# Causal attention on TensorE: the two heads of a pair in the two row halves of the array, and operand stacks loaded one stage earlier

## The chip, the cores and the metric

One Trainium2 (trn2) chip, one core. The metric is the device time of one execution in microseconds (us). The kernel before ran three times: 6051.51, 6053.97 and 6059.97 us, median 6053.97 us.

## The reference

A small recurrent network of two kinds of layers over 4 sequences of 1024 tokens with 128 channels. The first part is a tiled attention, then a causal attention with rotary positions behind a layer norm and a short convolution, then a mixture of four experts, then a second causal attention without rotation; after that come six layers of local attention with a gated network. The change touches only the two causal attentions. What each of them computes, cut down:

```python
# B = 4 sequences, T = 1024 tokens, 16 heads of D = 8 channels
q, k, v = split(h @ attn_w)                       # per head
scores = jnp.einsum('bqhd,bkhd->bhqk', q, k) / jnp.sqrt(D)
causal = jnp.tril(jnp.ones((T, T), dtype=bool))
p = jax.nn.softmax(jnp.where(causal, scores, -1e30), axis=-1)
y = jnp.einsum('bhqk,bkhd->bqhd', p, v).reshape(B, T, C)
return y @ proj_w
```

## The kernel before, in words

Every layer is a stage: the five engines run their own programs, joined by semaphores, and a barrier of all engines ends the stage. The two causal attentions are the stages named ca0 and ca1 (function `causal_attention`, tiles ending in `_of_ca`). Each follows a stage `causal_inputs` (ci0, ci1), which projects queries, keys and values in 8 chunks of 512 tokens and writes queries and keys, each cut into three bf16 parts, to memory (`q_parts`, `k_parts`, the two DMAs of a chunk at line 469). ci0 rotates the values and takes longer per chunk than ci1.

The work of an attention stage goes by 16 groups: 4 sequences times 4 groups of 4 heads. For a group SyncE (SP) loads a stack of queries and a stack of keys: six products of the three parts (`PRODUCTS`), 8 rows each, lie one above the other in 48 of the 128 partitions, so that one bf16 matmul gives a nearly exact fp32 score of a head. Two further rows, from `SHIFT_ROW` = 64, hold the negated maximum of each query against ones in the keys, so the maximum is subtracted inside the same matmul. The rest of the 128 rows is zero. There are three slots of stacks (`RING_CA`). They are cleared at the start of the attention stage, slot 0 by VectorE (lines 843 to 846), slots 1 and 2 by GpSimd (lines 594 to 596), and only then loaded (lines 556 and 558, 13 DMAs per group).

TensorE does two things for each group with these stacks:

- Maxima, one group ahead: `maximum` (line 624) computes scores with queries as rows. A task fills one of two double banks of PSUM (`PAIR_BANK`), and VectorE reduces it (line 783). There are 20 tasks per group, of 4 heads with 128 or 256 keys or of 2 heads with 384 or 512. Where the tile lies on the diagonal, a second matmul of 128 columns adds the mask (line 627).
- Scores and weighted values: the group is walked in 12 units (`UNITS`; query half 0 with 4 key tiles, query half 1 with 8). `score` (line 677) computes keys by queries, one head per bank in a ring of three banks (`SCORE_BANKS`), with a mask matmul on the diagonal (line 680); ScalarE takes the exponential out of the bank (line 759, semaphore `raised`); `weigh` (line 691) multiplies with the values of the four heads, in four strips of 32 columns of the array, one unit late.

The order on TensorE is written out: scores of heads 0 and 1, then the tasks of `between(G, i, 0)`, scores of heads 2 and 3, `between(G, i, 1)`, then `weigh` of the unit before. `BETWEEN` says how many maxima tasks stand in each of the two places. At unit 8 the eight matmuls of `turn_rows` (line 635) turn the maxima of the next group into the two rows that SP places in its stack (line 564). In some units of the first two groups of a sequence the steps of `FINISH` (totals, spread, mix) of the sequence before are added.

The two waits the change touches: a score matmul of one head waits until the exponential that used its bank before, three heads back, is done, and each head raises `scored` by itself.

```python
for h in heads:
    n = (G * NU + i) * HG + h
    if n >= SCORE_BANKS:
        pe.wait_ge(raised, n - SCORE_BANKS + 1)
    to = ps[:, n % SCORE_BANKS, j:]
    last = nc.tensor.matmul(to, keys[:, h, kt * P:(kt + 1) * P], ...)
    if diagonal:
        last = nc.tensor.matmul(to[:, 0:P], k["ident_b"][:, :], ...)
    last.then_inc(scored, 1)
```

Of the kernel before, what the change touches and what calls it, by code (L numbers as in the profile page):

```python
# [13 lines left out]
P = 128  # L14
# [18 lines left out]
SHIFT_ROW = 64  # L33
STACK_LOADS = 16 * (2 * len(PRODUCTS) + 1)
# [339 lines left out]
def causal_inputs(nc, name, ps, h, weights, tables, q_parts, k_parts, vtok):  # L374
# [4 lines left out]
    with Stage(nc, name) as st:  # L379
# [6 lines left out]
        stored, v_out, chain = [st.sem(f"stored{n}") for n in range(4)], st.sem("v_out"), st.sem("chain")  # L386
        with nc.Block() as block:
# [76 lines left out]
            def _(sp):  # L464
                for c in range(NCH):
                    for n, dram in enumerate((q_parts, k_parts)):
                        slot = c % 2 * 2 + n
                        sp.wait_ge(low, 2 * c + n + 1)
                        sp.dma_start(dram[:, :, chunk(c)].rearrange("s p t -> p s t"),
                                     parts[:, slot]).then_inc(stored[slot], 16)  # L470
                for slot in range(4):
                    sp.wait_ge(stored[slot], 16 * (NCH // 2))

# [4 lines left out]
RING_CA = 3  # L478
# [34 lines left out]
def causal_attention(nc, name, ps, k, q_parts, k_parts, vtok, proj, out, residual):  # L513
# [6 lines left out]
    with Stage(nc, name) as st:  # L520
        stacks = [(st.sb(f"queries{s}", [P, HG, L], BF16), st.sb(f"keys{s}", [P, HG, L], BF16)) for s in range(RING_CA)]
# [5 lines left out]
        zeros = st.sb("zeros", [2, L], BF16)  # L527
# [3 lines left out]
        cleared, first_cleared, copied = st.sem("cleared"), st.sem("first_cleared"), st.sem("copied")  # L531
# [6 lines left out]
        def in_pair(n, heads, width):  # L538

            first = PAIR_BANK + n % 2 * 2  # L540
            if heads == HG and width == P:
                return ps[:, first:first + 1, :].rearrange("p a (h n) -> p (a h) n", n=P)
            if heads == HG:
                return ps[:, first:first + 2, :].rearrange("p a (h n) -> p (a h) n", n=width)
            return ps[:, first:first + 2, 0:width]

        with nc.Block() as block:

            @block.sync
            def _(sp):  # L550
                def load(G):
                    slot, first = G % RING_CA, G % GROUPS * HG * HD
                    for to, dram, side in zip(stacks[slot], (q_parts, k_parts), range(2)):
                        for r, product in enumerate(PRODUCTS):
                            of = dram[product[side], first:first + HG * HD, G // GROUPS * L:(G // GROUPS + 1) * L]
                            sp.dma_start(to[r * HD:(r + 1) * HD, :, :], of.rearrange("(h d) t -> d h t", d=HD))\
                                .then_inc(loaded[slot], 16)
                    sp.dma_start(stacks[slot][0][SHIFT_ROW:SHIFT_ROW + 2, :, :],
                                 zeros[:, :].unsqueeze(1).to_broadcast([2, HG, L])).then_inc(loaded[slot], 16)

                def place(G):
                    sp.wait_ge(rows_out, G + 1)
                    for h in range(HG):
                        sp.dma_start(stacks[G % RING_CA][0][SHIFT_ROW:SHIFT_ROW + 2, h, :], rows[2 * h:2 * h + 2, :])\
                            .then_inc(placed[G % RING_CA], 16)

                sp.wait_ge(first_cleared, 8)
                load(0)
                for G in range(1, RING_CA):
                    sp.wait_ge(cleared, 7 * G)  # L570
                    load(G)
                place(0)
                for G in range(ALL - 1):
                    if G and G + 2 < ALL:
                        sp.wait_ge(scored, HG * NU * G)
                        load(G + 2)
# [5 lines left out]
            def _(pool):  # L582
# [9 lines left out]
                for queries, keys in stacks[1:]:  # L592
                    for low in (QUAD, SHIFT_ROW, SHIFT_ROW + QUAD):
                        link(nc.gpsimd.memset(queries[low:low + QUAD, :, :], 0.0))  # L594
# [1045 lines left out]
```

## Time and profile before

| what | value |
|---|---|
| median of 3 runs | 6053.97 us (6051.51 to 6059.97) |
| the profiled execution | 6055.52 us, its span 6053.7 us |
| TensorE matmul (PE) busy | 5119.5 us, 85% of the span |
| VectorE (DVE) busy | 4008.1 us, 66% |
| ScalarE (ACT) busy | 3245.7 us, 54% |
| GpSimd (POOL) busy | 1801.1 us, 30% |
| ca0 | from the clearing at 461.9 us to the last exponential at 1094.5 us |
| ca1 | from 1686.9 us to 2319.9 us |

PE is the row of matmuls, PEld that of weight loads. A matmul's duration holds its way through the array, so consecutive matmuls overlap in the records: what one costs in a row of many is the distance of their starts. "128\*128" behind an operation is the part of the array it uses, rows by columns. In the timeline a row with x8 stands for eight instructions in a row, and its time is from the start of the first to the end of the last; the bracket at the end is the idle time before it and what ended it.

### The profile page before, as it was taken

Reading aid. Unit: us, or ns where it says so; the run is one execution under the profiler, and the core shown is the slowest. Engines: PE = TensorE matmul, PEld = TensorE weight load, DVE = VectorE, ACT = ScalarE, POOL = GpSimd, SP = SyncE. Lnnn points to the kernel's source line nnn. Section 1 sums busy time; section 2 is a strip of 40 time slices with the busy share of each in tenths; the row PEclk is TensorE's granted clock in tenths of the full one; section 3 lists DMA queues with packets and bytes.
Section 4 is the critical chain, followed back from the end, with each engine's and each line's share of the span. In section 5 each row is a group of like instructions: output and inputs, shape, how many; then the busy total and the mean of one; then the engine's idle time right before and its main releaser. Section 6 shows DMA issues by size and latency. Waiting matters only on the chain. (4 is left out here: it accounts for less than half of the span.)

```text
span 6053.7 us, 164948 instructions
## 1 busy us (share of the span) xinstructions
PE 5119.5 (85%) x72264; PEld 2980.0 (49%) x72592; DVE 4008.1 (66%) x4630; ACT 3245.7 (54%) x4392; POOL 1801.1 (30%) x1232
## 2 busy tenths in 40 slices
PE   6756999788769996998799979997999799979997
PEld 3422333333323332666366636663666366636663
DVE  5756666233366664887488748884888488848884
ACT  2323555322235554776377637763777367736773
POOL 0003000000030001555155515551555055505550
PEclk9988999899889998999899989998999899989998
DMA  0011110000011111111111111110111011101111
GB/s 24 0 48 33 23 23 18 21 0 0 29 39 23 24 21 38 38 38 34 34 39 39 34 33 38 38 38 32 38 38 38 30 37 38 39 31 37 37 37 40
DMA packets 87157, 186.93 MB, mean 31 GB/s; under 512 B 23216, under 2 KB 39088, under 8 KB 84272
## 3 DMA queue, kind: packets, MB, share of 16 engines
q1 hardware_dynamic: 86448, 176.44, 12.1%
q8 instruction: 572, 9.37, 0.6%
q14 instruction: 137, 1.12, 0.1%
HBM read 59.97 MB, written 14.68 MB: 12 GB/s over the span
## 5 line engine op out<-in xcount | busy, mean ns | idle before, releaser
L1327 POOL TENSOR_TENSOR part_of_local<-part_of_local,sine_of_local 128x512 f32<-128x512 f32 x768 | 960.2, 1273 | 1061.3 <-DVE sine_of_local L1264 1061.3
L783 DVE TENSOR_REDUCE top_of_ca<-ps 128x2 f32<-128x1024 f32 (+3 forms) x640 | 695.1, 1115 | 298.6 <-PE ps L627 207.2
L759 ACT ACTIVATE prob_of_ca<-ps 128x512 f32<-128x512 f32 (+3 forms) x1536 | 654.5, 495 | 422.6 <-PE ps L680 311.0
L1334 POOL TENSOR_TENSOR part_of_local<-part_of_local,inverse_of_local 128x1024 f32<-128x1024 f32 x384 | 722.5, 1903 | 139.7 <-DVE inverse_of_local L1296 139.7
L624 PE MATMUL ps<-keys_of_ca,queries_of_ca 128*128 128x512 bf16 (+3 forms) x1474 | 386.4, 332 | 180.6 <-DMA queries_of_ca<-zeros_of_ca 86.4
L1301 DVE TENSOR_REDUCE total_of_local<-prob_of_local 128x16 f32<-128x1024 f32 x192 | 234.3, 1220 | 421.2 <-ACT prob_of_local L1240 421.2
L1261 DVE TENSOR_TENSOR part_of_local<-ps,rope 128x1024 f32<-128x1024 f32 x384 | 466.2, 1214 | 40.7 <-ACT square_of_local L1208 40.7
L1264 DVE TENSOR_TENSOR sine_of_local<-ps,rope 128x1024 f32<-128x1024 f32 x384 | 465.7, 1213 | 0.0
L1100 PE MATMUL ps<-qkv,shifted 128*128 128x512 f32 x768 | 392.4, 635 | 82.1 <-POOL values_of_local L1337 78.5
L1110 PE MATMUL ps<-qkv,shifted 128*128 128x512 f32 x768 | 381.6, 620 | 84.9 <-ACT heads_out_of_local L1236 71.8
L677 PE MATMUL ps<-queries_of_ca,keys_of_ca 128*128 128x512 bf16 (+2 forms) x1464 | 404.0, 331 | 24.3 <-issue 10.8
L1186 PEld LDWEIGHTS ps<-prob_t_of_local,mixed_of_local 64*64 64x64 f32 x12288 | 335.0, 135 | 166.2 <-issue 156.7
L1195 PE MATMUL ps<-heads_out_of_local,wo 128*128 128x128 f32 x3072 | 387.6, 281 | 14.1 <-ACT heads_out_of_local L1236 13.7
L1186 PE MATMUL ps<-prob_t_of_local,mixed_of_local 64*64 64x32 f32 x12288 | 383.8, 221 | 16.0 <-issue 9.1
L1186 PE MATMUL ps<-prob_t_of_local,values_of_local 64*64 64x32 f32 x12288 | 382.0, 219 | 4.7 <-issue 4.2
L1195 PEld LDWEIGHTS ps<-heads_out_of_local,wo 128*128 128x128 f32 x3072 | 368.8, 197 | 16.8 <-ACT heads_out_of_local L1236 16.7
L1167 PE MATMUL ps<-qkv,shifted 128*64 128x512 f32 x1536 | 376.9, 607 | 0.1
L594 POOL MEMSET queries_of_ca<- 32x4096 bf16 x12 | 42.1, 3505 | 1106.1 <-POOLq L63 1105.5
L1226 ACT ACTIVATE keys_of_local<-ps 128x1024 f32<-128x1024 f32 x192 | 196.8, 1025 | 323.2 <-PE ps L1129 323.2
L1247 ACT ACTIVATE values_of_local<-ps 128x1024 f32<-128x1024 f32 x192 | 196.6, 1024 | 306.2 <-PE ps L1167 306.2
L1186 PEld LDWEIGHTS ps<-prob_t_of_local,values_of_local 64*64 64x64 f32 x12288 | 338.0, 135 | 6.8 <-issue 5.9
L691 PE MATMUL ps<-prob_of_ca,values_of_ca 128*32 128x512 f32 (+3 forms) x3072 | 332.5, 505 | 0.0
(207 smaller groups left out, 9928.3 us busy)
## 6 DMA issues: line engine op xcount, KB each, us to landing
mixed_of_local<-values_of_local SPq DMA_DIRECT2D x636, 128.0 KB, 2.4
mixed_of_local<-values_of_local SPq DMA_DIRECT2D x264, 64.0 KB, 2.0
queries_of_ca<-q_parts SPq DMA_DIRECT2D x192, 64.0 KB
keys_of_ca<-k_parts SPq DMA_DIRECT2D x192, 64.0 KB
qkv<-in_qkv SPq DMA_DIRECT2D x7, 1536.0 KB, 6.5
rope<-in_rope SPq DMA_DIRECT2D x7, 1024.0 KB, 9.0
q_parts<-parts_of_ci SPq DMA_DIRECT2D x16, 384.0 KB, 2.5
k_parts<-parts_of_ci SPq DMA_DIRECT2D x16, 384.0 KB, 2.5
```

Source lines behind the costliest of these rows:

```text
L624: last = nc.tensor.matmul(to[:, h, :], queries[:, first + h, qt * P:(qt + 1) * P], keys[:, first + h, lo:lo + width], start=True, stop=not ...
L677: last = nc.tensor.matmul(to, keys[:, h, kt * P:(kt + 1) * P], queries[:, h, qc * CH + j:(qc + 1) * CH], start=True, stop=not diagonal)
L759: nc.scalar.activation(prob[:, i % 2, h, j:], ps[:, n % SCORE_BANKS, j:], ACT.Exp, scale=scale).then_inc(raised, 1)
L783: nc.vector.reduce_max(top[:, slot, first:first + heads], in_pair(n, heads, width), AX_X)\
L1100: last = nc.tensor.matmul(two_banks(SCORE_SLOT)[:, a, :], xs[:, tokens(t)], w["qkv"][:, 0, chunk(a)], start=True, stop=True)
L1110: last = nc.tensor.matmul(two_banks(KEY_SLOT)[:, a, :], xs[:, tokens(t)], w["qkv"][:, 1, chunk(a)], start=True, stop=True)
L1186: last = nc.tensor.matmul(out, src[rows, t % RING * 2 + i // 2, p + e, :], prob_t[rows, p + e, i * WIN:(i + 1) * WIN], start=True, stop=True)
L1195: last = nc.tensor.matmul(two_banks(OUT_SLOT)[:, 0, 0:P], w["o"][:, p, :], heads_out[:, p, :], start=p == 0, stop=p == PAIRS - 1)
L1261: nc.vector.tensor_tensor(part[:, t % 2, side], by_head(slot), table(2 * side, t), ALU.mult).then_inc(parts, 1)
L1264: nc.vector.tensor_tensor(sine[:, side], by_head(slot), table(2 * side + 1, t), ALU.mult).then_inc(parts, 1)
L1327: nc.gpsimd.tensor_tensor(out, out, sine[:, side, :, (1 - to) * half:(2 - to) * half], ALU.add).then_inc(rotated, 1)
L1334: nc.gpsimd.tensor_tensor(part[:, t % 2, side], part[:, t % 2, side], by, ALU.mult).then_inc(scaled, 1)
```

## The change

The two heads of a pair are put into the two row halves of the array: a stack now has the even head of a pair in partitions 0 to 63 and the odd one in 64 to 127, and each main matmul of `maximum` and `score` uses 64 rows. In a maxima task head e of each pair writes bank e of the double bank. The mask matmuls keep all 128 rows and follow the two main matmuls of a pair. A pair of score matmuls waits once, for the bank of its second head, and `scored` is raised once per pair. A load has 26 DMAs of half the size (functions `load_stack`, and for the clearing `clear_stacks`); the clearing moves to GpSimd in the stage of inputs, and SP issues the loads of the first three groups there, behind the stores of chunks 3, 4 and 5.

```diff
-SHIFT_ROW = 64
-STACK_LOADS = 16 * (2 * len(PRODUCTS) + 1)
+ROW_HALF = 64
+SHIFT_ROW = 32
+RING_CA = 3
+STACK_LOADS = 16 * (4 * len(PRODUCTS) + 2)
...
+def clear_stacks(pool, nc, cleared, stacks, zeros):
+    link = Chain(pool, cleared)
+    link(nc.gpsimd.memset(zeros[:, :], 0.0))
+    for queries, keys in stacks:
+        for half in (SHIFT_ROW, ROW_HALF + SHIFT_ROW):
+            link(nc.gpsimd.memset(queries[half:half + QUAD, :, :], 0.0))
+            link(nc.gpsimd.memset(keys[half:half + QUAD, :, :], 0.0))
+            link(nc.gpsimd.memset(keys[half:half + 2, :, :], 1.0))
...
+def load_stack(sp, loaded, stacks, zeros, q_parts, k_parts, G):
+    slot, first = G % RING_CA, G % GROUPS * HG * HD
+    for to, dram, side in zip(stacks[slot], (q_parts, k_parts), range(2)):
+        for r, product in enumerate(PRODUCTS):
+            of = dram[product[side], first:first + HG * HD, G // GROUPS * L:(G // GROUPS + 1) * L]
+            of = of.rearrange("(j e d) t -> e d j t", e=2, d=HD)
+            row = r * HD + (2 if r * HD >= SHIFT_ROW else 0)
+            for e in range(2):
+                sp.dma_start(to[ROW_HALF * e + row:ROW_HALF * e + row + HD, :, :], of[e]).then_inc(loaded, 16)
...
 # causal_inputs, SyncE, behind the two stores of chunk c
+                    if 3 <= c < 3 + RING_CA:
+                        if c == 3:
+                            sp.wait_ge(cleared, 1 + 6 * RING_CA)
+                            for slot in range(4):
+                                sp.wait_ge(stored[slot], 16)
+                        load_stack(sp, fetched[c - 3], stacks, zeros, q_parts, k_parts, c - 3)
...
 # maximum
-                    for h in range(heads):
-                        last = nc.tensor.matmul(to[:, h, :], queries[:, first + h, qt * P:(qt + 1) * P],
-                                                keys[:, first + h, lo:lo + width], start=True, stop=not diagonal)
+                    for j in range(heads // 2):
+                        for e in range(2):
+                            half = slice(ROW_HALF * e, ROW_HALF * (e + 1))
+                            last = nc.tensor.matmul(to[:, e, j, :], queries[half, first // 2 + j, qt * P:(qt + 1) * P],
+                                                    keys[half, first // 2 + j, lo:lo + width], start=True, stop=not diagonal)
                         if diagonal:
-                            last = nc.tensor.matmul(to[:, h, width - P:], k["ident_b"][:, :], k["after_q"][:, :],
-                                                    start=False, stop=True)
+                            for e in range(2):
+                                last = nc.tensor.matmul(to[:, e, j, width - P:], k["ident_b"][:, :], k["after_q"][:, :],
+                                                        start=False, stop=True)
...
 # score
+                    n = (G * NU + i) * HG + heads[0]
+                    if n + 1 >= SCORE_BANKS:
+                        pe.wait_ge(raised, n + 1 - SCORE_BANKS + 1)
                     for h in heads:
-                        n = (G * NU + i) * HG + h
-                        if n >= SCORE_BANKS:
-                            pe.wait_ge(raised, n - SCORE_BANKS + 1)
...
+                        half = slice(ROW_HALF * (h % 2), ROW_HALF * (h % 2 + 1))
+                        last = nc.tensor.matmul(ps[:, (n + h % 2) % SCORE_BANKS, j:], keys[half, h // 2, kt * P:(kt + 1) * P],
+                                                queries[half, h // 2, qc * CH + j:(qc + 1) * CH], start=True, stop=not diagonal)
+                    if diagonal:
+                        for h in heads:
+                            last = nc.tensor.matmul(ps[:, (n + h % 2) % SCORE_BANKS, j:j + P], k["ident_b"][:, :],
+                                                    k["after_k"][:, :], start=False, stop=True)
+                    last.then_inc(scored, 1)
```

First place: TensorE, group 0, unit 8 (the first diagonal unit of query half 1) up to `turn_rows`. L677 (now L702) are score matmuls, L624 (now L648) maxima, the others with `sb_ident_b` the masks. Before:

```order
L677 MATMUL ps<-queries_of_ca,keys_of_ca 128x512
L680 MATMUL ps<-sb_after_k,sb_ident_b 128x128
L677 MATMUL ps<-queries_of_ca,keys_of_ca 128x512
L680 MATMUL ps<-sb_after_k,sb_ident_b 128x128
L624 MATMUL ps<-keys_of_ca,queries_of_ca 128x128
L627 MATMUL ps<-sb_after_q,sb_ident_b 128x128
L624 MATMUL ps<-keys_of_ca,queries_of_ca 128x128
L627 MATMUL ps<-sb_after_q,sb_ident_b 128x128
L624 MATMUL ps<-keys_of_ca,queries_of_ca 128x128
L627 MATMUL ps<-sb_after_q,sb_ident_b 128x128
L624 MATMUL ps<-keys_of_ca,queries_of_ca 128x128
L627 MATMUL ps<-sb_after_q,sb_ident_b 128x128
```

The same place now:

```order
L702 MATMUL ps<-queries_of_ca,keys_of_ca 128x512 x2
L706 MATMUL ps<-sb_after_k,sb_ident_b 128x128 x2
L648 MATMUL ps<-keys_of_ca,queries_of_ca 128x128 x2
L652 MATMUL ps<-sb_after_q,sb_ident_b 128x128 x2
L648 MATMUL ps<-keys_of_ca,queries_of_ca 128x128 x2
L652 MATMUL ps<-sb_after_q,sb_ident_b 128x128 x2
L702 MATMUL ps<-queries_of_ca,keys_of_ca 128x512 x2
```

The two main matmuls of a pair (64 rows each) stand together, and behind each such pair the two masks (128 rows). In one plain group, one without steps of `FINISH`, 32 pairs have masks behind them, and 23 times another pair of 64-row matmuls follows directly on the masks; 16 pairs have no masks.

Second place: SyncE in ci0 and at the start of ca0, as it is now (L505 are the stores of a chunk, L403 and L405 a load, L596 the placed rows). Before, the sixteen stores stood in a row, and the first three loads, of 13 DMAs each, followed in the attention stage.

```order
L505 DMA k_parts<-parts_of_ci 128x3x512
L403 DMA queries_of_ca<-q_parts 8x2x1024 x12
L403 DMA keys_of_ca<-k_parts 8x2x1024 x12
L405 DMA queries_of_ca<-zeros_of_ca 2x2x1024 x2
L505 DMA q_parts<-parts_of_ci 128x3x512
L505 DMA k_parts<-parts_of_ci 128x3x512
L403 DMA queries_of_ca<-q_parts 8x2x1024 x12
L403 DMA keys_of_ca<-k_parts 8x2x1024 x12
L405 DMA queries_of_ca<-zeros_of_ca 2x2x1024 x2
```

The first row is the last store of chunk 3; each load of 26 DMAs now stands ahead of the stores of the next chunk.

## Rows read from the trace of the kernel before

**Rows 1.** Windows of the two attention stages; columns: busy time of each engine, granted clock, DMA

```profile
461.90:492.30 30.40, 0.00 (x0) 0.00 (x0) 14.55 (x8) 0.00 (x0) 29.94 (x9) 0.50 0.19 31
492.30:524.10 31.80, 19.57 (x121) 9.15 (x124) 27.36 (x29) 2.30 (x2) 21.45 (x10) 0.92 0.27 47
524.10:1094.50 570.40, 520.17 (x4145) 224.54 (x4212) 364.81 (x372) 353.96 (x814) 5.64 (x14) 0.98 0.11 20
1686.90:1717.60 30.70, 0.01 (x1) 0.01 (x1) 14.55 (x8) 0.00 (x0) 30.19 (x9) 0.50 0.19 32
```

**Rows 2.** The waits of PE in 524.1 to 1094.5 us: us, times, longest

```profile
PE ps L624 <- ACT rows_of_ca L742: 17.6, 14, 1.3
...
PE ps L677 <- ACT prob_of_ca L759: 2.0, 6, 0.6
```

**Rows 3.** Timeline of ACT in a plain group: start, us, instruction

```profile
557.50 2.06 ACT L759 ACTIVATE prob_of_ca<-ps 128x512 f32<-128x512 f32 x4 [0.61 <-PE ps L680]
...
571.82 2.06 ACT L759 ACTIVATE prob_of_ca<-ps 128x512 f32<-128x512 f32 x4 [0.77 <-PE ps L677]
574.65 2.07 ACT L759 ACTIVATE prob_of_ca<-ps 128x512 f32<-128x512 f32 x4 [0.76 <-remote]
...
589.74 0.60 ACT L759 ACTIVATE prob_of_ca<-ps 128x512 f32<-128x512 f32 x1 [0.61 <-PE ps L680]
```

**Rows 4.** Timeline of PE and PEld, unit 6 of a group in ca0

```profile
717.91 0.11 PEld L677 LDWEIGHTS ps<-queries_of_ca,keys_of_ca 128*128 128x128 bf16 x2 [0.84 <-ACT prob_of_ca L759]
717.91 0.61 PE L677 MATMUL ps<-queries_of_ca,keys_of_ca 128*128 128x512 bf16 x2
...
718.79 0.59 PE L677 MATMUL ps<-queries_of_ca,keys_of_ca 128*128 128x512 bf16 x2
...
719.75 1.06 PE L691 MATMUL ps<-prob_of_ca,values_of_ca 128*32 128x512 f32 x8
```

**Rows 5.** Timeline of PE, a weigh between maxima and diagonal scores

```profile
703.04 0.38 PE L624 MATMUL ps<-keys_of_ca,queries_of_ca 128*128 128x512 bf16 x1
703.35 0.43 PE L691 MATMUL ps<-prob_of_ca,values_of_ca 128*32 128x128 f32 x8
703.71 0.34 PE L677 MATMUL ps<-queries_of_ca,keys_of_ca 128*128 128x384 bf16 x1
```

**Rows 6.** Local attention, timeline of PE: eight tiles of 64*32 at once

```profile
3020.69 1.48 PE L1156 MATMUL ps<-keys_of_local,queries_of_local 64*32 64x64 f32 x128
```

**Rows 7.** The same, where 128*64 gives way to 64*64

```profile
3023.01 1.03 PE L1167 MATMUL ps<-qkv,shifted 128*64 128x512 f32 x4
3023.97 0.26 PE L1186 MATMUL ps<-prob_t_of_local,mixed_of_local 64*64 64x32 f32 x4
```

**Rows 8.** Line 1167: duration of one in ns (least, median, most)

```profile
L1167 PE MATMUL ps<-qkv,shifted x1536: 589/592/1114, 2373.5 to 5906.3; 128*64 128x512 f32 x192
```

**Rows 9.** Start of ca0, timeline: clearing, first load, first maxima

```profile
461.88 3.50 POOL L594 MEMSET queries_of_ca<- 32x4096 bf16 x1 [461.42 <-POOLq L63]
...
480.43 2.04 SPq L556 DMA_DIRECT2D queries_of_ca<-q_parts  x6
...
490.88 0.65 SPq L558 DMA_DIRECT2D queries_of_ca<-zeros_of_ca  x1
...
492.34 0.29 PE L624 MATMUL ps<-keys_of_ca,queries_of_ca 128*128 128x128 bf16 x1 [44.69 <-DMA queries_of_ca<-zeros_of_ca]
```

**Rows 10.** Stores of ci0: least, median, most ns; first and last start

```profile
L469 SPq DMA_DIRECT2D q_parts<-parts_of_ci x16: 359/359/394, 386.5 to 1680.1; - x16
L469 SPq DMA_DIRECT2D k_parts<-parts_of_ci x16: 359/360/373, 391.3 to 1683.5; - x16
```

**Rows 11.** Start of ci1, and its chunk 4 and last chunk

```profile
1627.29 1.10 PE L396 MATMUL ps<-cur,sb_dq 128*128 128x512 f32 x2 [1.70 <-PEq L63]
...
1656.03 0.36 SPq L469 DMA_DIRECT2D k_parts<-parts_of_ci  x1
...
1683.49 0.36 SPq L469 DMA_DIRECT2D k_parts<-parts_of_ci  x1
```

More of the change, by code:

```diff
@@ L386, in causal_inputs @@
         stored, v_out, chain = [st.sem(f"stored{n}") for n in range(4)], st.sem("v_out"), st.sem("chain")
+        cleared, fetched = st.sem("cleared"), [st.sem(f"fetched{n}") for n in range(RING_CA)]
         with nc.Block() as block:
@@ L470, in _ @@
                                      parts[:, slot]).then_inc(stored[slot], 16)
+                    if 3 <= c < 3 + RING_CA:
[4 more added lines that the diff above has]
+                        load_stack(sp, fetched[c - 3], stacks, zeros, q_parts, k_parts, c - 3)
                 for slot in range(4):
                     sp.wait_ge(stored[slot], 16 * (NCH // 2))
+                for G in range(RING_CA):
+                    sp.wait_ge(fetched[G], STACK_LOADS)
+            @block.gpsimd
+            def _(pool):
+                clear_stacks(pool, nc, cleared, stacks, zeros)
 UNITS = [(qc, kt, max(0, kt - qc * 4) * P) for qc in range(2) for kt in range(4 * qc + 4)]
@@ L477 @@
 ALL = B * GROUPS
-RING_CA = 3
 SCORE_BANKS = 3
@@ L538, in in_pair @@
         def in_pair(n, heads, width):
[L540 to L545, printed above, removed]
+            pair = ps[:, PAIR_BANK + n % 2 * 2:PAIR_BANK + n % 2 * 2 + 2, 0:heads // 2 * width]
+            return pair.rearrange("p e (j n) -> p e j n", n=width)
         with nc.Block() as block:
@@ L550, in _ @@
             def _(sp):
[L551 to L559, printed above, removed]
                 def place(G):
@@ L563, in place @@
                     for h in range(HG):
-                        sp.dma_start(stacks[G % RING_CA][0][SHIFT_ROW:SHIFT_ROW + 2, h, :], rows[2 * h:2 * h + 2, :])\
+                        row = ROW_HALF * (h % 2) + SHIFT_ROW
+                        sp.dma_start(stacks[G % RING_CA][0][row:row + 2, h // 2, :], rows[2 * h:2 * h + 2, :])\
                             .then_inc(placed[G % RING_CA], 16)
[L567 to L571, printed above, removed]
                 place(0)
@@ L574, in _ @@
                     if G and G + 2 < ALL:
-                        sp.wait_ge(scored, HG * NU * G)
-                        load(G + 2)
+                        sp.wait_ge(scored, 2 * NU * G)
+                        load_stack(sp, loaded[(G + 2) % RING_CA], stacks, zeros, q_parts, k_parts, G + 2)
                     place(G + 1)
@@ L1460, in build_program @@
                 vtok = ctx.enter_context(nc.sbuf_tensor("vtok0", [P, NT, P], F32))
+                stacks, zeros = causal_stacks(nc, ctx, "ca0")
                 w = buffers(ctx, ["cq", "ck", "cv", "cqs", "cks", "cproj", "taps", "ln1"])
@@ L1482, in build_program @@
                 vtok = ctx.enter_context(nc.sbuf_tensor("vtok1", [P, NT, P], F32))
+                stacks, zeros = causal_stacks(nc, ctx, "ca1")
                 w = buffers(ctx, ["dq", "dk", "dv", "dproj"])
```

49 lines of the change are left out of this document (19 added, 30 removed).

## The prediction, made before the changed kernel was run

> **What bounds the kernel now.** I read the windows first: from the first exponential to the last, ca0 takes 570.4 us, PE is busy for 520.2 of them at a granted clock of 0.98 (its 2.4 GHz level almost throughout), DVE for 365 and ACT for 354 [rows 1]. The waits say the rest: in these 570 us PE's matmuls wait 2.0 us in all for an exponential and 17.6 us for the turned rows [rows 2]. So PE bounds this loop, by the distances of its starts. ca1 repeats it. A plain group takes 32.24 us, from the exponential at 557.50 to the one at 589.74; a unit in the middle, without masks, takes 2.83 us (571.82 to 574.65) [rows 3]. The other thing to see is the head of each stage: PE stands still for 30.4 and 30.7 us [rows 1] while the stacks are cleared and loaded [rows 9].
>
> **Prices.** Two 512-column matmuls take 0.59 us from the first start to the last end, and one lasts 0.38 [rows 4, 5]: their starts are about 0.215 us apart, 0.42 ns per column, so a mask of 128 columns costs 0.055. Where PE changes the shape of the tile it uses, time is lost: the maxima matmul started at 703.04 has streamed by 703.255, yet the first 32-column matmul starts at 703.35, 0.095 later [rows 5]. That changes columns only. A change of rows alone is in the trace too: the last of four 128\*64 matmuls ends at 3024.04, started one duration of 0.592 earlier, at 3023.45, and has streamed (512 columns of fp32, 0.427 us) by 3023.875; the first 64\*64 matmul starts at 3023.97, again 0.095 later [rows 7, 8]. Of these 0.095 us some 0.002 is what any start costs. I take **0.093 us per change between half rows and full rows**. Bounds: nothing below, since no row has 64\*128 against 128\*128; above, 0.147 us, which is what is left of 0.36 us from the small weigh to the next score after its two passes of 0.107 us [rows 5].
>
> Do the halves run side by side? 128 fp32 matmuls of 64 columns, in eight tiles of 64\*32, take 1.48 us from first start to last end [rows 6]. At 0.053 us each, four column tiles at a time and one row half after the other, they would stream for 1.71 us. They do run together. The second of a pair starts a little later: two 128-column weight loads back to back end 0.01 us apart (0.11 us for both, one taking 0.10) [rows 4]; I take 0.015 us per entry into half rows.
>
> **The loop, per plain group.** (a) 16 pairs of 512 columns without masks: 0.215 us saved on each, 3.4 us. (b) 32 pairs with masks, eight each of 128, 256, 384 and 512 columns. Before, 2 x (columns x 0.42 ns + 0.055): 0.22, 0.33, 0.43 and 0.54 us, in all 12.2 us. Now columns x 0.42 ns + 0.015 + 0.093 + 0.11: 0.27, 0.33, 0.38 and 0.43, in all 11.3 us; and 23 times PE goes back from the masks to half rows, 0.093 each, 2.1 us. That is 1.2 us more. A 128-column pair loses, only 512 columns gain. PE's own work: 3.4 - 1.2 = **2.2 us less**.
>
> (c) The new wait. With three banks a pair needs the exponential of the head two before its first to be over, so heads 2 and 3 cannot start before the exponential of head 0 ends. That chain is 0.38 us of matmul [rows 5], 0.60 of exponential [rows 3] and some 0.08 that I allow for the two semaphores: 1.06 us, and 1.27 with masks (0.093 + 0.11 more). PE has between the two pairs only its first pair and the tasks of the first place. Unit 6: 0.215 + 0.215, so it waits 0.63. Unit 4 the same. Unit 5 waits 0.9, because the copy of the sums stands ahead of its exponentials on ACT. Unit 7 has a masked task and waits 0.3; unit 0: 1.27 - 0.76 = 0.5; units 1 and 2 about 0.3 together at their first and second pair each, 0.5 in all; unit 8 0.1; units 3, 9, 10 and 11 nothing, their chains being short. That is 3.6 us, less 0.4 us of such waits that the old order had in my reckoning (rows 2 put less down to it): 3.2 us. Unit 6 as a check: 1.06 + second pair 0.215 + task 0.215 + 0.093 + weigh 1.00 = 2.58 us for 2.83. Behind the waiting score stand maxima and weigh; DVE and ACT wait longer in turn, but both have over 9 us per group to spare, so they set nothing.
>
> Sum per plain group 3.2 - 2.2 = +1.0; carrying the unit sums through, with the masks' delay of the exponential in units 0, 8 and 9, I get 33.4 for 32.24, **+1.15 us**. Groups with finishing steps change by as much, the last group (no maxima) by +0.5. Over 16 groups that is +18 us, over both stages **+37 us**.
>
> The rule in the Trainium skill, "TensorEngine Tiling (Array Packing)", Tiling Modes, speaks against this change: changing the tiling mode drains the engine, while a change of tile within a mode does not. The trace agrees, with 0.095 us each time. Without that rule the sum would be the first rival's, 5918; with it, 6043.
>
> **The early loads.** ca0: PE's first matmul at 492.34, the clearing begins at 461.88 [rows 9]; the stacks will be there and PE starts about 0.5 us in: -29.9 us. From there to the first exponential DVE is busy 27.4 of 31.8 us [rows 1] with the same reductions: unchanged. What it costs the stage of inputs: POOL clears with 18 memsets of half the columns, 1.75 us each by [rows 9], 33 us in all. SP issues a load as 26 DMAs of 0.34 us (six take 2.04 us [rows 9]) and two of 0.65: 9.5 us, and the stores behind it wait. In ci0 stores come every 4.75 us (386.5 and 391.3 are the first two [rows 10]); clearing is done at about 411, chunk 3 is stored at 420, the three loads fit between the chunks, no buffer of parts is needed in time before it is stored: 0. In ci1 PE starts at 1627.29, so POOL is done at about 1660.7, behind the last store of chunk 3 at 1656.03; stores come every 3.43 us [rows 11]. Load 0 lasts till 1670.3, load 1 till 1680.5, load 2 till 1690.8; chunk 6 waits for the store of chunk 4 (2.4 us), chunk 7 for that of chunk 5 (5.8 us in all), and the last transfers land near 1697 instead of 1686: +10.5. PE stood still for 30.7 us here [rows 1], and 0.5 stay, so ca1 gains 30.2 - 10.5 = 19.7. Later loads (9.5 us of SP instead of 4.7 in a group of 33) stay ahead of the maxima that read them by some 10 us, and the placed rows behind them too: 0. The early loads are worth **-49 us** (bounds -42 to -56: a load's DMAs at 0.26 or at 0.40 us, and a landing of 3 to 7 us).
>
> **Sum.** 6055.5 (the profiled execution) + 37 - 49 = 6043. The execution lies 1.5 us above the median of the runs, which is nothing here. The gain and the loss nearly cancel; one part in 500, 12 us, is about what a measurement of this kernel tells from no change, and the forecast stands at that line.
>
> **Rivals.**
> 1. *The change of rows costs nothing or little* (chance 0.12). At 0 the 55 added changes of a group go: the unit sums give 44 us less per stage than before, time 6055.5 - 88 - 49 = 5918; at half price 5980. For it: no row has 64\*128 tiles, and rows need not cost what other shapes do. Against it stand the 0.095 us of a change of rows alone [rows 7]. The Trainium skill, "TensorE: Matmul & The Clock Gate", Part 3: Packing small matmuls, lets each further tile start about 4 ns after the one before and names no price for leaving the mode.
> 2. *Slower: each entry into half rows costs 0.04 us more* (chance 0.25), the second tile's 128-column weight load starting when the first has passed, 0.055 instead of 0.015 later, or the change itself at 0.13. Place: the 36 entries of a group. 36 x 0.04 x 32 groups = 46 us, less what falls into waits: the loop adds 75 to 80 instead of 37, time 6085. It turns the sign at about 0.01 us per entry and is told from no change from 0.02 on. For it: full-array starts never come closer than 0.055 us, and the way back from the weigh costs up to 0.147 [rows 5]. Against: the two weight loads 0.01 apart [rows 4].
> 3. *The halves run one after the other* (chance 0.03): no stream is saved, 7.7 us per group come back, less 1.8 of waits: 6043 + 190 = 6233. Against: rows 6.
> The forecast keeps 0.60, its own range 6015 to 6070 (changes at 0.08 to 0.105 us, which is 12 us per stage, and the bounds of the early loads).
>
> **Numbers.** Below 6042 lie half of the forecast (0.30) and rival 1 (0.12), together 0.43 with the edge of rival 2; within 12 us two fifths of the forecast and a part of rival 2, 0.27; above 6066 the rest, 0.30. The range that leaves out one in ten on each side goes from 5960, inside rival 1, to 6100, behind rival 2.
>
> **What would show it.** Right: PE's first maxima in ca0 within 1 us of the barrier, ci0 as long as before and ci1 10 us longer; two 512-column starts of a pair 0.015 us apart, the next pair 0.22 later; 0.09 us between a half-row stream's end and its mask; unit 6 at 2.6 us, unit 9 at 4.4, a plain group at 33.4; PE's waits for exponentials up from 2 us to some 50 per stage. Wrong: a plain group under 32 us (changes cheaper than 0.06 us) or over 34.5 (entries dearer), ci0 longer by more than 3 us, or a granted clock in the loop below 0.95 in place of 0.98.

## The result, and the profile after

The changed kernel takes 6092.1 us (median of 6 runs, 6075.8 to 6094.6) where the kernel before took 6057.0 beside it (6 runs): ratio 1.0050, 95% interval 1.0035 to 1.0065. It is slower, by 35 us between the medians and by 30 as the ratio gives it, where 12 us less were forecast. 6092 lies within the wide range of the prediction (5960 to 6100) but above the forecast's own range (6015 to 6070). The profiled execution spans 6090.3 us for 6053.7.

Windows of the changed kernel: the head of ca0 (from the first maxima to the first exponential), its loop, its last group, and head and loop of ca1. Columns as in [rows 1].

```profile
466.20:498.30 32.10, 24.60 (x126) 7.61 (x126) 27.30 (x29) 2.29 (x2) 2.33 (x4) 0.50 0.00 1
498.30:1105.70 607.40, 519.43 (x4205) 168.00 (x4212) 368.39 (x373) 362.00 (x813) 5.60 (x14) 0.94 0.07 19
1070.60:1105.70 35.10, 27.29 (x171) 6.34 (x172) 0.00 (x0) 21.40 (x49) 0.00 (x0) 0.66 0.01 1
1710.50:1742.60 32.10, 24.57 (x126) 7.61 (x126) 27.28 (x29) 2.29 (x2) 2.33 (x4) 0.50 0.01 2
1742.60:2343.10 600.50, 512.25 (x4206) 167.55 (x4212) 368.43 (x373) 361.95 (x813) 5.60 (x14) 0.96 0.07 19
```

The last group of ca0 in the kernel before:

```profile
1069.60:1094.50 24.90, 21.62 (x168) 6.90 (x172) 0.00 (x0) 20.36 (x50) 0.00 (x0) 1.00 0.00 1
```

Both loops are longer, 607.4 and 600.5 us for 570.4, with PE as busy as before but at a lower granted clock: 0.94 and 0.96 for 0.98, 0.66 for 1.00 in the last group. In the head it is 0.50 for 0.92. The low level of the head reaches 8.5 us into the loop:

```profile
498.30:506.80 8.50, 8.20 (x40) 1.94 (x40) 4.87 (x5) 4.33 (x10) 0.00 (x0) 0.50 0.00 0
```

By stretches, from starts in the two traces:

| stretch, us | before | after | forecast |
|---|---|---|---|
| ci0, first to last store | 71.7 | 71.8 | 0 |
| to the first maxima of ca0 | 34.2 | 3.6 | -29.9 |
| head of ca0 | 31.8 | 31.8 | 0 |
| loop of ca0 | 570.4 | 607.4 | +18 |
| ci1, first to last store | 51.5 | 64.0 | +10.5 |
| to the first maxima of ca1 | 34.1 | 5.5 | -30.2 |
| head of ca1 | 31.8 | 31.8 | 0 |
| loop of ca1 | 570.4 | 600.5 | +18 |

The early loads gave 46.6 us (49 forecast), the loops took 67 (37 forecast): +20. The other 16 us of the two spans lie in stages that the change leaves alone (386.5 and 391.2 us before ci0, 3733.9 and 3747.2 after ca1, less 1.8 between ca0 and ci1). In the traces of the experiments the first two of these stretches take 385 to 396 and 3722 to 3754 us in no order that follows the kernel, so I take them for scatter; below I compare stretches of the stages in question, and medians beside them. What the stages in question account for is 20 us of the loss, not all 30 to 35.

PE's waits in the loop of ca0, as [rows 2]:

```profile
PE ps L702 <- ACT prob_of_ca L786: 36.9, 88, 0.9
PE ps L648 <- ACT rows_of_ca L769: 20.6, 14, 1.5
```

PE and then ACT in a plain group of ca0 (534.46 to 568.19, 33.7 us; granted clock 1.00), as [rows 3 to 5]:

```profile
541.93 0.28 PE L706 MATMUL ps<-sb_after_k,sb_ident_b 128*128 128x128 bf16 x2
542.15 0.28 PE L648 MATMUL ps<-keys_of_ca,queries_of_ca 64*128 64x256 bf16 x2
542.36 0.28 PE L652 MATMUL ps<-sb_after_q,sb_ident_b 128*128 128x128 bf16 x2
542.58 0.28 PE L648 MATMUL ps<-keys_of_ca,queries_of_ca 64*128 64x256 bf16 x2
...
543.96 0.39 PE L702 MATMUL ps<-queries_of_ca,keys_of_ca 64*128 64x512 bf16 x2
544.19 0.38 PE L648 MATMUL ps<-keys_of_ca,queries_of_ca 64*128 64x512 bf16 x2
545.05 0.39 PE L702 MATMUL ps<-queries_of_ca,keys_of_ca 64*128 64x512 bf16 x2 [0.48 <-ACT prob_of_ca L786]
```

```profile
534.46 1.08 ACT L786 ACTIVATE prob_of_ca<-ps 128x512 f32<-128x512 f32 x2 [0.67 <-PE ps L706]
...
549.73 2.17 ACT L786 ACTIVATE prob_of_ca<-ps 128x512 f32<-128x512 f32 x4 [0.61 <-PE ps L702]
552.35 2.17 ACT L786 ACTIVATE prob_of_ca<-ps 128x512 f32<-128x512 f32 x4 [0.45 <-PE ps L702]
...
568.19 1.08 ACT L786 ACTIVATE prob_of_ca<-ps 128x512 f32<-128x512 f32 x2 [0.67 <-PE ps L706]
```

Two 512-column streams now take 0.39 us from first start to last end, as one did: the halves run together (the second starts 3 to 4 ns after the first), and pair follows pair 0.23 us later. The price stands in the second to fourth line of PE: a pair of 256 columns streams 0.107 us, but its masks start 0.21 after it, 0.10 late; the masks stream 0.11 and the next pair starts 0.22 after them, 0.11 late. One masked pair of 256 columns costs 0.43 us, where two heads one after the other took 0.33.

SP in ci1:

```profile
1665.43 0.36 SPq L505 DMA_DIRECT2D k_parts<-parts_of_ci  x1
1670.99 4.04 SPq L403 DMA_DIRECT2D queries_of_ca<-q_parts  x12
1675.07 4.05 SPq L403 DMA_DIRECT2D keys_of_ca<-k_parts  x12
1679.17 1.41 SPq L405 DMA_DIRECT2D queries_of_ca<-zeros_of_ca  x2
1680.62 0.40 SPq L505 DMA_DIRECT2D q_parts<-parts_of_ci  x1
...
1705.35 1.09 SPq L505 DMA_DIRECT2D k_parts<-parts_of_ci  x1
```

Clearing ends 5.5 us behind the start of the last store of chunk 3, at 1665.43 (4.7 forecast); then each load keeps SP for 9.6 to 10.5 us, and the last store is 40 us behind that of chunk 3 for 27.5 before.

### The profile page after: what moved, and what is told of

It reads as the page before. It is cut to its first block and busy times, and to the rows that moved or that the text cites. A ratio compares the mean times of both kernels' runs of the same rounds, so it can differ in the third digit from the quotient of the medians.

```text
span 6090.3 us, 165482 instructions
## 1 busy us (share of the span) xinstructions
PE 5145.0 (84%) x72386; PEld 2875.4 (47%) x72592; DVE 3987.8 (65%) x4614; ACT 3262.0 (54%) x4392; POOL 1769.4 (29%) x1242
## 5 line engine op out<-in xcount | busy, mean ns | idle before, releaser
L786 ACT ACTIVATE prob_of_ca<-ps 128x512 f32<-128x512 f32 (+3 forms) x1536 | 673.8, 490 | 472.9 <-PE ps L706 363.6
L648 PE MATMUL ps<-keys_of_ca,queries_of_ca 64*128 64x512 bf16 (+3 forms) x1536 | 273.1, 352 | 137.9 <-ACT rows_of_ca L769 41.3
L718 PE MATMUL ps<-prob_of_ca,values_of_ca 128*32 128x512 f32 (+3 forms) x3072 | 348.5, 527 | 0.0
L615 POOL COPY values_of_ca<-vtok 128x256 f32<-128x256 f32 x32 | 12.7, 400 | 1132.7 <-PE ps L718 1132.5
L702 PE MATMUL ps<-queries_of_ca,keys_of_ca 64*128 64x512 bf16 (+3 forms) x1536 | 267.6, 345 | 79.1 <-ACT prob_of_ca L786 74.6
```

The lines of the kernel that those rows point to most:

```text
L718: last = nc.tensor.matmul(ps[h * QUAD:(h + 1) * QUAD, SUM_BANK, j:], values[:, G % 2, kt, h, :], prob[:, i % 2, h, j:], start=kt == 0, sto ...
L786: nc.scalar.activation(prob[:, i % 2, h, j:], ps[:, n % SCORE_BANKS, j:], ACT.Exp, scale=scale).then_inc(raised, 1)
```

## Experiments

Each ratio is to the kernel before, run beside the experiment; its median there was 6063 to 6066 us. Theory: the loss lies in the loops. Changes of rows at the masks cost 0.10 us each, which the waits for exponentials do not absorb, and TensorE's granted clock, which the sum had left at 0.98, is lower with the halves. Rivals: the wait of a pair sets the loop; the early loads give less than figured. "Plain group" is the distance of the first exponentials of two groups without finishing steps.

### 1. The halves alone

The stacks are cleared and loaded in the attention stage, as before; the rest is the change.

```
+                sp.wait_ge(first_cleared, 7)
+                load(0)
+                for G in range(1, RING_CA):
+                    sp.wait_ge(cleared, 6 * G)
+                    load(G)
                 place(0)
```

> The halves and their layout alone; stacks cleared and loaded in the attention stage, as in the kernel before. Theory A (the loss lies in the loop: half rows and full rows change at every mask, pairs wait, and TensorE's granted clock is lower there): a plain group 33.7 us as in the change, the loops 30 to 37 us longer than before, PE idle for 25 to 30 us at the head of each stage (fewer columns to clear); time 6057 + 67 - 5 + up to 15 = 6115 to 6135. Theory C (the early loads give less than 49 us because they lengthen the stage of inputs or delay the loop): under 6100. Both agree on the plain group.

Measured: 6107.9 us, ratio 1.0068 (1.0054 to 1.0082). Plain group 33.7, both loops 602.8 (+32.4 each), 24.6 and 24.3 us to the first maxima. By these stretches +45 us: +65 of the loops, -20 because half as many columns are cleared. The time lies between the two theories' ranges (6115 to 6135, and under 6100), the stretches are as Theory A says: the loss is in the halves. The early loads on top of them are worth 25 us by the stretches (45 against 20), 11 by the ratios.

### 2. The early loads alone

Full rows and the old loop; the stacks belong to both stages and are cleared and loaded in the stage of inputs.

```
+                    if 4 <= c < 4 + RING_CA:
+                        if c == 4:
+                            sp.wait_ge(cleared, 1 + 5 * RING_CA)
+                        ...
+                        load_stack(sp, fetched[c - 4], stacks, zeros, q_parts, k_parts, c - 4)
```

> The early loads alone, full rows and one wait per head as in the kernel before; clearing in 16 memsets of 3.5 us (two wide ones for a tensor in place of three), the loads put behind chunks 4, 5 and 6, since clearing takes 54 us here. Theory A: the plain group stays at 32.2 us and the loops at 570, ca0 gains 30, ca1 some 12 to 18 (clearing ends behind the last store): 6057 - 42 to 48, 6009 to 6015. Theory C: 6035 or more, by a longer ci0 or a longer loop.

Measured: 6023.9 us, ratio 0.9939 (0.9925 to 0.9953). The loop of ca0:

```profile
499.20:1069.30 570.10, 522.49 (x4146) 223.67 (x4212) 365.82 (x374) 353.85 (x813) 5.60 (x14) 0.97 0.12 20
```

Plain group 32.2, loops 570.1 and 567.4, ci0 71.7, but ci1 70.1 us for 51.5, so that only 6 us of the gain at ca1 stay. SP waits there for the end of the clearing, 19 us behind the last store of chunk 4. From the first store of each stage of inputs to the first exponential 38 us are gained in all, a few short of the 42 expected; the time lies between the two theories. So one half of the change is good, and the other spoils it. The two do not add up (-39 and +45 us against +30 to 35 for both): each holds a part of the clearing that is saved only once.

### 3. The wait and the report of a pair alone, in full rows

```
+                    if (G * NU + i) * HG + heads[1] >= SCORE_BANKS:
+                        pe.wait_ge(raised, (G * NU + i) * HG + heads[1] - SCORE_BANKS + 1)
                     for h in heads:
                         n = (G * NU + i) * HG + h
-                        if n >= SCORE_BANKS:
-                            pe.wait_ge(raised, n - SCORE_BANKS + 1)
                         ...
-                        last.then_inc(scored, 1)
+                    last.then_inc(scored, 1)
```

> The kernel before with only the wait of the change: both heads of a pair wait together for their banks, and their scores are reported once, in full rows. It bounds what the waiting is worth. Theory A: PE's waits for exponentials go from 2 us to some 40 to 50 a stage, plain group 35 us, loops 40 us longer each, time 6135; a pair wait is dear where the second head of a pair does not run beside the first. Theory B expects the same or more. If the wait costs nothing here (6060), it explains nothing in the change.

Measured: 6152.0 us, ratio 1.0151 (1.0136 to 1.0166). Plain group 35.5, loops 615 (45 longer, 40 expected). PE's waits in the loop of ca0:

```profile
PE ps L677 <- ACT prob_of_ca L759: 28.8, 85, 0.9
...
PE ps L677 <- issue: 5.4, 31, 0.3
```

28.8 us for 2.0, under the 40 to 50 expected, yet the group grew as forecast: these rows do not hold all that the wait costs. The granted clock stays at 0.98 here, though PE is idle for 81 us of this loop and was for 50 before: waits of this size in full rows do not lower it.

```profile
523.80:1138.90 615.10, 533.64 (x4146) 219.10 (x4210) 370.52 (x372) 362.13 (x813) 5.60 (x14) 0.98 0.10 18
```

### 4. All masks in half rows

Each head's mask is added by two matmuls of 64 rows in that head's half. Three constants with swapped halves are added.

```
                         if diagonal:
-                            for e in range(2):
-                                last = nc.tensor.matmul(to[:, e, j, width - P:], k["ident_b"][:, :], k["after_q"][:, :],
+                            for a in (QTR, 0):
+                                for e in range(2):
+                                    half, swap = slice(ROW_HALF * e, ROW_HALF * (e + 1)), "_s" * (e == (a == 0))
+                                    last = nc.tensor.matmul(to[:, e, j, width - P + a:], k["ident_b" + swap][half, :],
+                                                            k["after_q" + swap][half, a:], start=False, stop=a == 0)
```

> The change with its masks in half rows too: each head's mask is two matmuls of 64 rows (64 and 128 columns) in that head's own half, from three more constants with swapped halves; no change of rows is left between a pair and its mask. Theory A: the 55 changes of 0.10 us and 0.03 us of each mask pair leave a group, some 6 us of PE's work, of which more waits for exponentials eat 2: plain group 29.9, loops 59 us shorter than in the change, time about 5975; up to 20 us more if the granted clock falls below 0.94. Theory B (the wait of a pair for the exponential of head 0 sets the loop): plain group not under 32.5, time 6050 or more.

Measured: 5952.5 us, ratio 0.9821 (0.9807 to 0.9835). The loop of ca0, and a masked pair:

```profile
490.60:1030.80 540.20, 424.09 (x5180) 158.36 (x5184) 364.62 (x373) 362.10 (x814) 5.63 (x14) 0.96 0.08 21
```

```profile
534.29 0.33 PE L649 MATMUL ps<-keys_of_ca,queries_of_ca 64*128 64x384 bf16 x2
534.46 0.19 PE L655 MATMUL ps<-sb_after_q_s,sb_ident_b_s 64*128 64x64 bf16 x1
534.46 0.24 PE L655 MATMUL ps<-sb_after_q,sb_ident_b 64*128 64x64 bf16 x2
```

The first masks start 0.17 us after a pair that streams 0.16: next to nothing is lost any more. (The masks are also shorter and run side by side, 0.03 us a pair as expected above, 1 us of a group.) Plain group 30.0 for 29.9 expected, loops 540.1 and 535.4. PE waits 60.5 us for exponentials here, more than in the change, and the kernel is 140 us faster, with the wait of a pair still in it: that wait does not set the loop of the change. It beats both kernels.

### 5. Only the masks of the maxima in half rows

Experiment 4, with the masks of the scores put back:

```
                     if diagonal:
-                        for b in (QTR, P):
-                            ...
+                        for h in heads:
+                            last = nc.tensor.matmul(ps[:, (n + h % 2) % SCORE_BANKS, j:j + P], k["ident_b"][:, :],
+                                                    k["after_k"][:, :], start=False, stop=True)
```

> Only the masks of the maxima in half rows, those of the scores in full rows as in the change. Theory (each change has its price and both kinds cost alike): 16 of the 32 masked pairs of a group lose theirs, plain group 32.1 between 33.7 and 30.0, loops 27 us shorter than the change's, time about 6030. Rival (the masks of the scores alone matter, since they stand in the chain to the exponentials): over 33 us and 6070.

Measured: 6023.0 us, ratio 0.9930 (0.9915 to 0.9946). Plain group 32.2, loops 569.9 and 571.9. The two kinds of masks pay back 1.5 and 2.2 us of a group: both count, those of the scores somewhat more.

### 6. More changes of rows

The change with a wait and a mask per head at the scores.

```
                     for h in heads:
+                        n = (G * NU + i) * HG + h
+                        if n >= SCORE_BANKS:
+                            pe.wait_ge(raised, n - SCORE_BANKS + 1)
                         ...
+                        if diagonal:
+                            last = nc.tensor.matmul(ps[:, n % SCORE_BANKS, j:j + P], k["ident_b"][:, :],
+                                                    k["after_k"][:, :], start=False, stop=True)
+                        last.then_inc(scored, 1)
```

> The change, with each head of a pair waiting for its own bank and followed by its own mask, as in the order before: at the scores a masked pair now changes rows four times in place of two and its streams no longer run side by side; at the maxima nothing is changed. A test of the price per change by more of them. Theory (0.10 us each, in sum): 16 masked pairs of a group with two changes more, 0.2 us, and up to 0.17 us of lost overlap each, less the waits for exponentials: plain group 37.4 for 33.7, loops about 54 us longer than in the change, time near 6195. Rival (changes cost little, the joint wait made the change slow): plain group at or under 33.7, time 6090 or less.

Measured: 6234.6 us, ratio 1.0268 (1.0249 to 1.0287). Where the clock is full a plain group takes 37.5 us, as expected. (Besides the changes of rows this edit takes away the overlap of the masked pairs at the scores; the two are not told apart.) Much of the rest is clock: groups 0 to 2 of ca0 take 49.4, 49.1 and 45.2 us. The first two and the whole loop:

```profile
501.00:599.50 98.50, 95.95 (x521) 27.60 (x521) 46.08 (x47) 47.44 (x101) 0.40 (x1) 0.66 0.03 10
501.00:1191.10 690.10, 640.93 (x4210) 214.79 (x4214) 367.96 (x373) 375.47 (x813) 5.63 (x14) 0.89 0.06 17
```

PE is busy for 96 of 98.5 us by its records, and is granted 0.66. The last groups of ca0 and ca1 hold the same instructions and differ in the clock:

```profile
1151.20:1191.10 39.90, 38.82 (x170) 9.37 (x173) 0.00 (x0) 22.10 (x49) 0.00 (x0) 0.55 0.00 1
2465.30:2492.70 27.40, 25.29 (x170) 8.66 (x173) 0.00 (x0) 21.50 (x49) 0.00 (x0) 1.00 0.01 1
```

### 7. More work in the last group

```
-    return range(first, min(first + BETWEEN[i][slot], ALL * NM))
+    return range(first, first + BETWEEN[i][slot] * (G + 1 < ALL or first + BETWEEN[i][slot] <= (ALL + 1) * NM))
```

> The change, with more work put into the last group of each stage: a further set of maxima (of a stack that is still there, used by nobody) is computed in it, so that it becomes like the others. Clock theory (the last group, 35.1 us at a granted clock of 0.66 where it took 24.9 at 1.00 before, is long because the clock falls while PE has only scores and weighing): the added work is free or better, last group 33 to 35 us at a clock near 1.00, time 6085 to 6095. Rival (its length is its chain of waits and changes): with the maxima it grows by 7 us a stage as plain and last group differed before (32.2 and 24.9), 42 us, time 6105 or more.

Measured: 6079.6 us (12 runs), ratio 1.0024 (1.0013 to 1.0035), against 1.0050 for the change. The last groups of ca0 and ca1:

```profile
1066.30:1095.70 29.40, 24.67 (x220) 7.51 (x218) 15.77 (x14) 21.41 (x50) 0.00 (x0) 1.00 0.00 1
2306.50:2335.90 29.40, 24.67 (x220) 7.52 (x218) 15.77 (x14) 21.40 (x49) 0.00 (x0) 1.00 0.01 1
```

More matmuls and fourteen reductions more, and the group takes 29.4 us in place of 35.1 and 30.3, at 1.00. (Measured to the last exponential, as the 24.9 of before; "33 to 35" was a distance from group to group, and the edit adds 14 of a group's 20 tasks.) With experiment 6, where the same last group takes 39.9 us at 0.55 and 27.4 at 1.00, this shows that the extra length was the clock. The gain of the whole is small: the edit also gives the missing maxima to the group before the last, which takes 33.7 and 35.1 us for 31.2, so the last two groups together gain 3 us in ca0 and lose 3 in ca1, and both loops together are 1.4 us shorter (602.9 and 603.6 us). The ratios, whose intervals touch, do not show more than that.

### 8 and 9. Twice the streams in the head

The pairs of the maxima in the head are issued twice, in the change and in the kernel of experiment 6.

```
-                        for e in range(2):
+                        copies = 1 + (m < NM + AHEAD)
+                        for e in (0, 1) * copies:
                             ...
```

> The change, with every pair of streams of the maxima in the head of each stage issued twice (the second writes the same over the first). Clock theory (in the head the granted clock stays at 0.50, where it was 0.92 before, because PE streams too little there with two heads side by side, and what is held down then runs into group 0): with more streaming the clock rises within the head, and group 0 takes 33.7 to 34.5 us in place of 36.1; the head itself 31.8 us, since DVE sets it, or up to 3 us more until the clock has risen; time within 5 us of 6092. Rival (the clock stays at 0.50 whatever is streamed, or follows the time since the idle stretch): head 35 us or more, group 0 still 36, time 6097 or more.

> The same doubling in the kernel with a wait and a mask per head, where the 1.2 GHz level of the head lasted through groups 0 to 2 (49.4, 49.1 and 45.2 us where a plain group took 37.5). Clock theory: groups 0 to 2 take 37.5 to 40 us, the first loop is 25 to 35 us shorter, time 6190 to 6210 for 6235. Rival (the clock falls because of the loop's own changes of rows, not of where it starts): groups 0 to 2 stay above 45 us.

Measured: 6085.1 us, ratio 1.0036 (1.0023 to 1.0050), and 6216.2, ratio 1.0242 (1.0224 to 1.0260). Head and group 0 of ca0 and the head of ca1 in the first of them:

```profile
470.00:504.20 34.20, 28.89 (x190) 8.06 (x190) 27.12 (x29) 2.31 (x3) 2.31 (x4) 0.67 0.00 1
504.20:537.80 33.60, 29.29 (x258) 9.83 (x258) 23.44 (x24) 22.29 (x51) 0.00 (x0) 1.00 0.01 2
1709.90:1741.80 31.90, 24.20 (x190) 7.45 (x190) 26.99 (x29) 2.32 (x3) 2.32 (x4) 0.88 0.01 2
```

The clock rises within the head, and group 0 takes 33.6 us for 36.1, as expected; the head pays 2.4 us for it in ca0 and nothing in ca1. Neither time can be told from that of the same kernel without the doubling (1.0050, and 1.0268 in experiment 6, with overlapping intervals); the reading rests on the groups. In the second kernel groups 1 and 2 of ca0 fall to 37.5 us, but group 0 still takes 47.2, and in ca1 group 1 takes 46.1: there the clock also falls in the loop itself. Neither theory holds alone for that kernel.

### 10. A wait per head, with the masks of a pair behind both

Against experiment 4:

```
                     for h in heads:
+                        n = (G * NU + i) * HG + h
+                        if n >= SCORE_BANKS:
+                            pe.wait_ge(raised, n - SCORE_BANKS + 1)
                         ...
+                        if not diagonal:
+                            last.then_inc(scored, 1)
```

> All masks in half rows, and each head waits for its own bank and is reported by itself, with the masks of a pair still behind both. Bank theory (what costs is that three banks let only one head of the second pair start before the exponential of head 0 ends; waiting jointly adds nothing): plain group 29.5 to 30.3 for 30.0, time 5945 to 5960. Rival (the joint wait costs, as 3.3 us per group in full rows): plain group under 29, time under 5930.

Measured: 5945.9 us, ratio 0.9815 (0.9798 to 0.9832). Plain group 29.7: the joint wait is worth 0.3 us here, while it cost 3.3 in full rows. The time cannot be told from experiment 4.

### 11. One set of stacks, cleared once

Against experiment 4:

```
+                    start = 3 if rotated else 2
+                    if start <= c < start + RING_CA:
...
+                if rotated:
+                    clear_stacks(pool, nc, cleared, stacks, zeros)
```

> All masks in half rows, and one set of stacks for both stages, cleared once; in the second stage of inputs nothing is cleared and the loads stand behind chunks 2, 3 and 4. Theory (that stage is 12.5 us longer in the change because clearing ends late and the loads of 10 us stand before the last stores): it is 51.5 to 54 us long again for 64, its head stays as it is, time 5952 - 11 to 14 = 5940. Rival (SP's 28 us of issues lengthen it wherever they stand): 60 us or more, time 5948 or more.

Measured: 5951.3 us, ratio 0.9804 (0.9787 to 0.9822). ci1 takes 59.6 us for 64.0, more than the 54 expected: three loads of 10 us within 34 us still hold up the stores. Both causes were there, and the time cannot be told from experiment 4.

### 12. What the runs would keep

Experiments 7, 10 and 11 together, and in the stages of inputs only the load of the first group.

```
+                for G in range(1, RING_CA):
+                    load_stack(sp, loaded[G], stacks, zeros, q_parts, k_parts, G)
                 place(0)
```

> What the runs so far would keep: all masks in half rows, a wait per head, one set of stacks cleared once, in the stages of inputs only the load of the first group (those of the second and third stand at the start of the attention stage), and the further set of maxima in the last group. Theory: plain group 29.7, both stages of inputs as long as before (71.7 and 51.5 us), heads within 5 us, last group 26 us: 5946 - 12 for the second stage of inputs, - 3 to 8 for the last groups, about 5930 (5920 to 5945). Rival (the loads of the second and third group now come late for their maxima, 20 us of SP in a head of 29): first groups or heads longer by 5 us or more each, time 5945 or more.

Measured: 5924.8 us (5905.4 to 5926.9), ratio 0.9764 (0.9750 to 0.9777), the fastest of all. ci0 71.7 and ci1 51.9 us, plain group 29.7, last groups 26.5. The loads of the second and third group are in time: the heads take 29.2 and 29.6 us, the first groups 29.8 and 31.0.

## Why the prediction was wrong

- **Price of a change**: right. 0.093 us was forecast, the trace shows 0.10 to 0.11, and the halves start side by side. The Trainium skill, "TensorEngine Tiling (Array Packing)", Tiling Modes, says that a change of mode drains the engine; the trace agrees in that 0.10 us or more go at each change, and whether it drains is not seen in it. Experiments 4 and 5 answer with -3.7 and -1.5 us per group to fewer changes, experiment 6 with +3.8 to more of them and less overlap.
- **Plain group**: 33.4 forecast, 33.7 measured; unit 6 2.62 for 2.58, unit 9 4.43 for 4.4. The near hit is in part luck, since two terms missed in opposite ways: in the group shown PE's rows have 2.4 us of waits for exponentials, not the 3.2 counted, and with them its own work fell by 0.9 us, not 2.2. A masked pair that another pair follows costs 0.015 us more than figured (0.105 into the masks, 0.099 back, 0.066 from the first mask to the second), some 0.4 us of a group; the rest was not traced. Rival 2 came near the time, 6085 for 6092, but by a mechanism that was not measured: entries at 0.04 us more would give a plain group over 34.5.
- **The new wait**: PE waits 37 us for exponentials in the loop of ca0, not some 50. By these rows the term was too dear, as said; experiment 3 shows that they can leave out a part.
- **Early loads**: 46.6 us for 49. ca0 gave 30.5 for 29.9, ca1 16.1 for 19.7, by a stage of inputs 12.5 us longer, not 10.5, and 5.5 us, not 3.9, from its last store to the maxima.
- **The step that failed** is "over 16 groups that is +18 us": the loop as 16 groups at an unchanged granted clock of 0.98. It measured +37 and +30. Lost clock explains up to (0.98 - 0.94) x 607 = 24 us and (0.98 - 0.96) x 600 = 12 us, where the excess is 19 and 12. Group by group: the last took 35.1 and 30.3 us for 25.4 forecast, the first was 2.7 and 2.2 us longer than before, and three and two plain groups took 35.1 or 35.2 instead of 33.7. "The last group (no maxima) by +0.5" was the worst single term, 9.7 us off in ca0. "Groups with finishing steps change by as much" failed too, in both directions: groups 4, 8 and 12 stay at 47.5 to 47.8 us, and groups 5, 9 and 13 take 40.6 for 38.2, at 0.96 for 1.00 (39.2 where the clock is full, in experiment 1). Why the former do not grow is open. The text had named a clock under 0.95 as a sign of being wrong, but had put no price on it.
- The forecast was a small difference of two large terms (+37 and -49), and 30 us more on the first turned its sign. Experiments 6 to 8 show the clock's part for the last and the first group. The falls in between (35.1-us groups) were seen, not provoked, and what makes the clock fall stays open. 10 to 15 us of the measured loss lie in no stage that the change touches.

## What to carry to other kernels

Before packing two matmuls side by side, count what stands between the pairs in another tile shape: with the masks in full rows this kernel lost 30 us, with them in half rows it gained 110 (both with the early loads). When a change makes PE stream less in the same time, price the granted clock, above all where PE waits for another engine (heads) or has lost a kind of its work (last groups). It is not settled by the kernel alone: the same last group got 0.55 in ca0 and 1.00 in ca1 of experiment 6. And split a mixed change into its parts: here one alone was worth -39 us, the other alone +45.

## What was not expected of the hardware

The granted clock does not follow PE's busy share in the records. In the head of ca0 PE is busy 24.6 of 32.1 us at 0.50, where before it was busy 19.6 of 31.8 at 0.92 [rows 1]; in experiment 6 it is busy 96 of 98.5 us at 0.66. Part of this is circular, for records are longer at the low level: the 258 matmuls of group 0 are busy 32.3 us at 0.88 in the change and 29.3 at 1.00 in experiment 8. The Trainium skill, "TensorE: Matmul & The Clock Gate", Part 1, lets the clock follow how busy PE has been; read as the profile's busy time, that doesn't hold here. What changed in the head is that the same maxima are streamed by two heads at once, so that their own streams, without the masks, take about half as long; with these streams doubled the clock came back to 0.67 in ca0, and to 0.88 in ca1. Added work thus made groups shorter, by 5.7 us in the last group of ca0 and 2.5 in the first, though what it took elsewhere (in the group before the last, and in the head of ca0) ate much of that. Whether rows in use or streaming time decides was not tried.
